# Joined products, sums and small steps on VectorE and GpSimd, and rows and bias added by accumulating DMAs, in a fused autocorrelation-attention and feed-forward kernel

## What is computed

```
x = x + autocorrelation(layernorm(x), ctx, ctx)            # x, ctx: (8, 512, 2048), 8 heads
    # per head and channel:
    qf, kf = fft(q, axis=positions), fft(k, axis=positions)
    corr = ifft(qf * conj(kf)).real
    w, idx = top_k(corr, 12);  w = softmax(w)
    out = sum_i w_i * v[min(idx_i + position, L - 1)]
h = layernorm(x)
out = h @ W.T + bias + sum_e coeffs_e * scales_e * (h @ A_e.T) @ B_e.T      # W: (2048, 2048), 16 experts of rank 16
x = x + out
```

## Time and profile before

| what | value |
|---|---|
| median of 3 runs | 2646.56 us (2642.76 to 2648.35) |
| profiled execution: span of the core | 2644.4 us |
| profiled execution: its own time beyond the span | not shown by the page |
| mean granted TensorE clock | 0.984 |
| DMA | 613.19 MB, 232 GB/s over the span |

### The profile page before, as it was taken

The page is one execution under the profiler, slowest core; times in us unless marked ns, Lnnn a source line. Parts: engine busy times, 40 slices in busy tenths (PEclk is TensorE's granted clock), DMA queues, the critical chain, the costliest instruction groups (busy, mean ns, idle before and its releaser), DMA issues.

```text
span 2644.4 us, 36606 instructions
## 1 busy us (share of the span) xinstructions
PE 2497.7 (94%) x12288; PEld 1559.9 (59%) x12288; DVE 1901.7 (72%) x4966; ACT 1055.7 (40%) x1906; POOL 2155.5 (82%) x1558
## 2 busy tenths in 40 slices
PE   4999866799999999999999999999999999999998
PEld 3655555566666656666666666666666666654444
DVE  5989989778787788777877788778876688645000
ACT  4788855533443343533443334533333233201000
POOL 5799999778998799988998899888998899654222
PEclk8999978899999999999999999999999999999999
DMA  9399998966788687966887687957786687758853
GB/s 325 99 261 269 269 244 198 231 192 209 254 266 228 219 252 238 277 203 210 258 270 210 217 275 248 271 181 236 253 250 172 219 265 243 199 203 301 268 180 114
DMA packets 550028, 613.19 MB, mean 232 GB/s; under 512 B 322640, under 2 KB 448720, under 8 KB 532176
## 3 DMA queue, kind: packets, MB, share of 16 engines
q1 hardware_dynamic: 549840, 610.86, 76.6%
HBM read 383.22 MB, written 151.00 MB: 202 GB/s over the span
## 4 chain that ended last, share of the span: by engine, by line
PE 53%; POOL 22%; DVE 8%; DMA 7%; SPq 5%; issue 4%; ACT 1%; POOLq 0%; DVEq 0%; ACTq 0%
PE f_ps L840 11%; PE f_ps L844 11%; PE f_ps L842 11%; PE a_ps L718 7%; PE a_ps L805 5%; PE a_ps L763 4%; POOL a_zu L1115 4%; POOL f_x1p L1115 4%; POOL a_rows L1115 3%; DMA a_w_lag<-a_w_row 2%; PE a_ps L821 2%; PE a_ps L820 2%; POOL a_zv L1115 2%; POOL a_zf L1115 2%; PE a_ps L768 1%
## 5 line engine op out<-in xcount | busy, mean ns | idle before, releaser
L840 PE MATMUL f_ps<-f_whi,f_hhi 128*128 128x512 f16 x2048 | 777.3, 380 | 5.6 <-issue 2.4
L844 PE MATMUL f_ps<-f_whi,f_hlo 128*128 128x512 f16 x2048 | 777.4, 380 | 0.0
L842 PE MATMUL f_ps<-f_wlo,f_hhi 128*128 128x512 f16 x2048 | 777.4, 380 | 0.0
L924 ACT ACTIVATE a_side<-a_ps 128x256 f32<-128x256 f32 (+1 forms) x320 | 128.0, 416 | 873.5 <-PE a_ps L805 698.4
L844 PEld LDWEIGHTS f_ps<-f_whi,f_hlo 128*128 128x128 f16 x2048 | 200.6, 98 | 242.3 <-issue 1.1
L842 PEld LDWEIGHTS f_ps<-f_wlo,f_hhi 128*128 128x128 f16 x2048 | 200.7, 98 | 230.8 <-issue 1.1
L840 PEld LDWEIGHTS f_ps<-f_whi,f_hhi 128*128 128x128 f16 x2048 | 200.7, 98 | 220.6 <-issue 6.7
L1115 POOL TENSOR_TENSOR a_prod<-a_prod,a_tf 128x512 f32<-128x512 f32 x128 | 160.2, 1273 | 138.7 <-DVE a_tf L1242 138.7
L1115 POOL TENSOR_TENSOR a_zv<-a_zv,a_tw 128x512 f32<-128x512 f32 x128 | 183.3, 1450 | 100.5 <-DVE a_tf L1242 100.5
L805 PE MATMUL a_ps<-inv,a_prod 128*128 128x256 f32 x1024 | 239.5, 388 | 25.6 <-POOL a_prod L1115 25.6
L1115 POOL TENSOR_TENSOR f_x1p<-f_x1p,f_y 128x512 f32<-128x512 f32 x128 | 172.7, 1381 | 101.0 <-DVE f_y L1242 101.0
(11 more groups left out here) (137 smaller groups left out, 5236.6 us busy)
## 6 DMA issues: line engine op xcount, KB each, us to landing
f_whi<-whi_scratch SPq DMA_DIRECT2D x128, 512.0 KB, 5.1
f_wlo<-wlo_scratch SPq DMA_DIRECT2D x128, 512.0 KB, 6.5
a_rows<-in_x_dram SPq DMA_DIRECT2D x62, 1024.0 KB, 8.7
vs<-in_ctx_dram SPq DMA_DIRECT2D x64, 512.0 KB, 6.2
xs<-in_x_dram SPq DMA_DIRECT2D x64, 512.0 KB, 8.0
parts_scratch<-a_so SPq DMA_DIRECT2D x64, 512.0 KB, 7.5
x_scratch<-a_rows SPq DMA_DIRECT2D x32, 1024.0 KB, 5.1
f_x1p<-x_scratch SPq DMA_DIRECT2D x32, 1024.0 KB, 6.8
```

Of the source, the lines that this page charges most:

```text
L840: nc.tensor.matmul(f_ps[:, t, :], h_hi[q][:, kq, rows_t], w_hi[u % WR][:, :, kq, :], start=(k == 0), stop=False)
L842: nc.tensor.matmul(f_ps[:, t, :], h_hi[q][:, kq, rows_t], w_lo[u % WR][:, :, kq, :], start=False, stop=False)
L844: mm = nc.tensor.matmul(f_ps[:, t, :], h_lo[q][:, kq, rows_t], w_hi[u % WR][:, :, kq, :], start=False, stop=(k == DB - 1))
L924: return nc.scalar.activation(out, source, ACT.Copy, **how)
```

## The change

The spectra of values (vk) and of the upper part (uk) are kept side by side in one tile of six blocks, so that one VectorE instruction multiplies a PSUM bank with both halves it is needed for: multiply_queries and multiply_upper issue two products of 1024 elements each in place of four of 512, multiply_lower two of 2048 in place of eight. ScalarE writes the first copy of a spectrum in one instruction with 1024 elements. On GpSimd add_upper loses its raise (the one-partition add of the last row), add_lower adds in two instructions of 1024, raises both parts in one, and adds the halves in one. In largest and choose the small steps over the two halves of a chunk are one instruction each, and each fold of the lags as well; their semaphores count once a chunk. The attn and bias buffers go. add_row and add_bias are DMAs from GpSimd's queue that accumulate into the tile, from parts and from bias in DRAM. x1p and scale have two buffers, and load_group waits for group g-1 where it waited for group g. The core of the diff:

```diff
             def store_x1(w, r):
-                sp.wait_ge(row_added, r + 1)
+                sp.wait_ge(row_added, 16 * (r + 1))
...
-                at_least(sp, y_done, TB * g)
-                sp.dma_start(scale_sb[:, :], wscale[cols].partition_broadcast(T)).then_inc(scale_in, 16)
-                at_least(sp, bias_added, g)
-                sp.dma_start(bias_sb[:, :], bias[cols].partition_broadcast(T)).then_inc(bias_in, 16)
-                at_least(sp, out_out, 16 * g)
+                x1p = x1ps[g % 2]
+                at_least(sp, y_done, TB * (g - 1))
+                sp.dma_start(scales_sb[g % 2][:, :], wscale[cols].partition_broadcast(T)).then_inc(scale_in[g % 2], 16)
+                at_least(sp, out_out, 16 * (g - 1))
...
-                if r is not None and r % TB == 0:
-                    load_attn(r, False)
...
                     store_x1(w, r)
-                    if r % TB < TB - 1:
-                        load_attn(r + 1, True)
...
-                copy(dst[:, 1:3, :], ps[:, 2, :, :])
-                copy(dst[:, 0, :], ps[:, 2, 0, :]).then_inc(moved, 1)
+                copy(dst.rearrange("p (r j) c -> p r j c", j=2)[:, 0:3:2],
+                     ps[:, 2, :, :].unsqueeze(1).broadcast_to([T, 2, 2, CH])).then_inc(moved, 1)
...
             def add_lower(n):
...
+                sums, parts_z = by_pair(z[:, 4:12, :]), by_pair(terms[:, :, :], 6)
+                add(sums[:, :, 0], parts_z[:, :, 0], ALU.add).then_inc(zf_added, 1)
+                add(sums[:, :, 1], parts_z[:, :, 1], ALU.subtract).then_inc(z_paired, 1)
                 pool.wait_ge(zu_added, n + 1)
+                pool.wait_ge(zf_added, n + 1)
                 pool.wait_ge(last_raised, n + 1)
...
+                add(z[0:1, 0:9:8, :], last[n % LB][0:1, :].unsqueeze(1).broadcast_to([1, 2, CH]), ALU.add
+                    ).then_inc(zu_raised, 1)
                 pool.wait_ge(z_paired, n + 1)
                 pool.wait_ge(zu_raised, n + 1)
-                add(zu[:, 0:2, :], zv[:, 0:2, :], ALU.add)
-                add(zu[:, 2:4, :], zv[:, 2:4, :], ALU.add).then_inc(z_added, 1)
+                add(zu, zv, ALU.add).then_inc(z_added, 1)
...
                 pool.wait_ge(rows_in[w % 2], 16 * rows_job(w))
-                pool.wait_ge(attn_in, 16 * (r + r // TB + 2))
-                add(rows[w % 2][:, :], attn[:, :], ALU.add).then_inc(row_added, 1)
+                at_least(pool, row_added, 16 * r)
+                pool.wait_ge(parts_out, 16 * CHUNKS * (r // TB + 1))
+                pool.dma_start(rows[w % 2][:, :], part_rows[r * T:(r + 1) * T, :], accum_op=ALU.add
+                               ).then_inc(row_added, 16)
...
-                pool.wait_ge(x1p_in, 16 * (g + 1))
-                pool.wait_ge(bias_in, 16 * (g + 1))
-                add(x1p[:, :, :], bias_sb[:, :].unsqueeze(1).broadcast_to([T, TB, WC]), ALU.add
-                    ).then_inc(bias_added, 1)
+                cols = slice(g % 4 * WC, (g % 4 + 1) * WC)
+                pool.wait_ge(x1p_in[g % 2], 16 * (g // 2 + 1))
+                pool.dma_start(x1ps[g % 2][:, :, :], bias[cols].partition_broadcast(T).unsqueeze(1).broadcast_to([T, TB, WC]),
+                               accum_op=ALU.add).then_inc(bias_added, 16)
...
+            def product_by_both(out, bank, both):
+                source = ps[:, bank, :, :].rearrange("p j c -> p (j c)").unsqueeze(1).unsqueeze(1)
+                return product(out, source.broadcast_to([T, 2, 2, 2 * CH]),
+                               both.rearrange("p s (r j) c -> p s r (j c)", j=2))
...
             def multiply_lower(n):
...
+                product_by_both(by_pair(z[:, 4:12, :]), 2, both[:, :, 0:4, :]).then_inc(w0_used, 1)
                 dve.wait_ge(w0_mm, 2 * n + 2)
                 dve.wait_ge(prod_added, 2 * min(n + 2, N))
...
+                product_by_both(by_pair(terms[:, :, :], 6), 3, both[:, :, 2:6, :]).then_inc(w0_used, 1)
...
             def choose(n):
...
+                dve.wait_ge(far_copied, SUB * (n + 1))
+                by_lag = ps[:, 0:2, :, :].rearrange("p g h (a l) -> p (g h) a l", a=2)
+                copied = side[:, :, :].rearrange("p g (h l) -> p (g h) l", h=2)
+                near, far = by_lag[:, :, 0, 1:T], by_lag[:, :, 1, 1:T]
+                nc.vector.tensor_tensor(far, near, copied[:, :, 1:T], ALU.subtract)
+                nc.vector.tensor_tensor(near, near, copied[:, :, 1:T], ALU.add).then_inc(lags_folded, 1)
```

More of the change, by code:

```diff
@@ L171, in inverse_root_of_tile, with by_pair @@
         op.then_inc(link, 1)
+def by_pair(tile, every=4):
+    return tile.rearrange("p (s a) c -> p s a c", a=every)[:, :, 0:4, :].rearrange("p s (r j) c -> p s r (j c)", j=2)
 class Shared:
@@ L274, in flow @@
         y = sb("f_y", [T, TB, WC])
-        x1p = sb("f_x1p", [T, TB, WC])
-        scale_sb = sb("f_scale", [T, WC])
-        bias_sb = sb("f_bias", [T, WC])
+        x1ps = [sb(f"f_x1p{i}", [T, TB, WC]) for i in range(2)]
+        scales_sb = [sb(f"f_scale{i}", [T, WC]) for i in range(2)]
         f_bn = sb("f_bn", [T, 4, 6])
@@ L287, in flow @@
         idle = sb("a_idle", [1, 8])
-        tq = sb("a_tq", [T, TB, CH])
         tv = sb("a_tv", [T, TB, CH])
[L290 to L295, removed]
+        spectra = [sb(f"a_spectra{i}", [T, 2, 6, CH]) for i in range(2)]
+        z = sb("a_z", [T, 12, CH])
+        zu, zv, zf = z[:, 0:4, :], z[:, 4:8, :], z[:, 8:12, :]
         tu = sb("a_tu", [T, 4, CH])
-        tw = sb("a_tw", [T, 4, CH])
-        tf = sb("a_tf", [T, 4, CH])
-        term = tf
+        terms = sb("a_terms", [T, 12, CH])
+        prod = terms[:, 4:12, :]
+        tq = terms[:, 0:4, :]
         wts = sb("a_wts", [T, SUB, L])
@@ L425, in flow @@
         y_added = sem("f_y_added")
-        x1p_in = sem("f_x1p_in")
-        scale_in = sem("f_scale_in")
-        bias_in = sem("f_bias_in")
+        x1p_in = [sem(f"f_x1p_in{i}") for i in range(2)]
+        scale_in = [sem(f"f_scale_in{i}") for i in range(2)]
         bias_added = sem("f_bias_added")
@@ L1154, in add_products @@
                 pool.wait_ge(q_used, 2 * (n + 1))
-                add(prod[:, 0:2, :], term[:, 0:2, :], ALU.add).then_inc(prod_added, 1)
-                add(prod[:, 2:4, :], term[:, 2:4, :], ALU.subtract).then_inc(prod_added, 1)
+                add(prod[:, 0:2, :], prod[:, 4:6, :], ALU.add).then_inc(prod_added, 1)
+                add(prod[:, 6:8, :], prod[:, 2:4, :], ALU.subtract).then_inc(prod_added, 1)
             def add_upper(n):
@@ L1318, in choose @@
                                                    ).then_inc(kept, 1)
[L1319 to L1331 removed]
+                dve.wait_ge(kept, SUB * (n + 1))
+                nc.vector.tensor_scalar(total, total, 1.0 / LAG_SCALE, None, ALU.mult).then_inc(total_scaled, 1)
+                dve.wait_ge(total_scaled, n + 1)
+                nc.vector.reciprocal(share, total).then_inc(share_known, 1)
+                dve.wait_ge(far_copied, SUB * (n + 1))
[4 more added lines that the diff above has]
+                nc.vector.tensor_tensor(near, near, copied[:, :, 1:T], ALU.add).then_inc(lags_folded, 1)
             def weights_low(n):
```

110 lines of the change are left out of this document (35 added, 75 removed).

## The result

The changed kernel takes 2775.99 us, the median of 4 runs (2774.88 to 2777.8), beside 2644.66 for the kernel before in the same session: 1.0495 times as long, 95% interval 1.048 to 1.051, or 131 us more. The prediction had said 2664 with a range that ended at 2702. The sign was right, the size was a seventh of what came.

What follows compares the result with a forecast made beforehand. It took a chain of full TensorE windows as the bound, broken by lag matmuls waiting for transposed weights. 2644.4 + 25 - 3 - 3 - 2 = 2661 us of span, 2664 as run median; range 2620 to 2702.

Steps and rivals of the forecast that it cites:

- Part (3): Bias by accumulating DMA: about 11 us of cover before the group add, costed at nothing; GpSimd 1.2 us earlier.
- part (2): VectorE's joined products and sums: nothing net, bound 1.2 us either way in each of the first 12 windows.
- parts (1): GpSimd's small adds joined: 0.5 us less a window, hidden in the middle, 3 us gained over seven early windows.
- Rival C: Bias lands late, after more than 11 us, delaying group add, output matmuls and row: +50 to +80; chance 0.10.
- Part (4): Rows by accumulating DMA: late sum makes TensorE wait 3.1 us in second and fourth row tiles; cost 25 us.
- D: Time from GpSimd reaching the row to the semaphore freeing SyncE and VectorE: 4.5 us before, taken as 9.0.
- Part (5): Ends: 3 us gained from 340 to 490 us, 2 us less after 2300 us.
- the even waits of 3 us at the lags: Expected sign: lag matmuls wait about 3 us each in second and fourth row tiles alike, clock dips behind.
- all of GpSimd's 320 us: Expected sign: GpSimd's busy time falls by some 290 us of row and bias adds and 30 of joined ones.
- waits appear in front of the group add: Sign of being wrong: waits in front of GpSimd's group add, which the bias DMA was expected to precede.
- plain windows change length: Sign of being wrong: windows without a row tile were expected to stay at 36.30 us.
- rivals A: Slower by the late row, landing in about 8.3 to 11 us; up to +52, 2698 us; chance 0.46.

Runs made afterwards that it cites:

- e4: The changed kernel with the bias DMA issued one window earlier: 2716.1 us.
- e1: The changed kernel with the negated maximum and the scaled total as two 128x1 instructions each again: 2745.5 us.
- e7: The kernel before with only the row of the residual added by an accumulating DMA: 2684.5 us.
- e3: The changed kernel with the bias added on GpSimd again from single buffers, rows still by accumulating DMA: 2721.9 us.
- e2: The changed kernel without both accumulating DMAs, rows and bias added on GpSimd as before, everything joined kept: 2685.7 us.
- e13: The changed kernel with the two small steps on 128x1 again and the bias DMA issued one window earlier: 2690.9 us.
- e6: The changed kernel without both accumulating DMAs and with the small steps on 128x1, leaving wide products and joined adds: 2642.0 us.
- e8: The kernel before with the weights' transposes issued ahead of the store of x1 on SyncE: 2665.7 us.
- e5: The kernel before with only the negation and the scaling joined, each once on 128x2: 2888.0 us.
- e10: e6 with the negation and scaling joined to 128x2 as products with a tile of constants: 2715.6 us.
- e9: e7 with the part output placed ahead of the row statistics on VectorE: 2726.7 us.

## Why the prediction was wrong

The 131 us are three shares, each from a run that undoes it: the late bias 62 us (e4), the two small steps 33 (e1), the row's DMA 36 to 47 (e7, e3 against e2, e13 against e6). The wide products and joined adds give back 5 (e6). Part (3) is the largest miss, part (2) the one with the wrong mechanism.

**Part (2), "I set all of (2) at nothing net; the bound is 1.2 us either way", is the step with the wrong mechanism.** It bounded each joined step by the fixed part of an instruction, so joining could save 1.2 us or cost a short delay. The two steps on 128x2 cost 1.7 us in each of the first windows and 33 in all, and alone in the kernel before 241. Its count was high too: twelve and seven instructions less a window, where the page shows 15 in all. The neighbours of the term were right: e6 is at -5 where parts (1) and (2) without these steps gave -3, the joined 128x1024 add takes 2350 ns where 2.35 us were worked out, and the raise of 512 elements 1255 ns where 715 + 500 were.

The trace before did hold the row that I needed, in a group that I had not read. VectorE's row remainder (L1394), in the kernel before, once beside GpSimd and once with its second input in PSUM:
```profile
L1394 DVE TENSOR_TENSOR f_rowlo<-a_rows,f_rowhi x28: 2281/2328/5586, 658.4 to 2458.9; 128x2048 f16<-128x2048 f32 x28
L1394 DVE TENSOR_TENSOR f_rowlo<-a_rows,f_ps x4: 2278/2278/2280, 379.3 to 476.2; 128x2048 f16<-128x2048 f32 x4
```
(least, median and greatest duration in ns.) With an input in PSUM the four take 2278 to 2280; with both inputs in SBUF it goes up to 5586, and in e8 to 13048. One instance on each engine, kernel before:
```profile
1544.51 3.45 DVE L1394 TENSOR_TENSOR f_rowlo<-a_rows,f_rowhi 128x2048 f16<-128x2048 f32 x1
...
1540.87 4.93 POOL L1115 TENSOR_TENSOR f_x1p<-f_x1p,f_y 128x512 f32<-128x512 f32 x4
1545.77 4.54 POOL L1115 TENSOR_TENSOR a_zu<-a_zu,a_tu 128x512 f32<-128x512 f32 x2
```
GpSimd's add ends at 1545.80, and VectorE's operation 2.16 us after that, nearly the 2.28 that it takes alone. GpSimd's next pair takes 4.54 in place of 2.50: it waited in turn. The Trainium skill says why in "SBUF — State Buffer", Who interferes with whom: VectorE and GpSimd share a pair of ports under an exclusive lock. A VectorE operation with two inputs in SBUF contends with a GpSimd instruction that reads SBUF, and one in a two-port mode, which tensor_scalar can enter, takes the pair for its whole length. By that rule the products out of PSUM stay free, and the joined small steps and the row remainder need not. The traces agree with it in e1, e5, e8 and e10. The page has the other engine block while the first one holds the pair; e5 shows VectorE passed over for five GpSimd instructions in a row.

**Part (3), "I cost it at nothing; its cover is gone if it lands later than that", had a cover but no duration.** The cover of about 11 us was near: GpSimd issued at 1064.81 and wanted the sum at 1074.7, 9.9 us. But I gave the bias no landing time, and took its being in time for the likeliest. It lands after 13.8 us. Rival C has exactly this mechanism and price (+50 to +80; measured 62), and I gave it a chance of 0.10 without a duration to weigh. The row's 8.5 us do not hold for it: same bytes, other shape.

**Part (4) had the right D, two thirds of the price, and the wrong place.** D = 9.0 against 8.9 in the tile above and a median of 8.5. +25 against 36 alone. That e7's two waits also grew by 25 us is chance: the prediction's 25 were 19 us of waits and 6 of clock, measured are 25 of waits and 14 of clock. The estimate from the Trainium skill, D near 11 by "Collectives: The Full Stack", is above the medians that the runs show, 8.0 to 9.1; the 7 from "DMA: Bandwidth & Descriptors", in the Trainium skill too, is below them. The wait did not come at the lags, about 3 us in each second and fourth tile, but at the queries, since VectorE's part output is queued behind the statistics. I had named VectorE among those that wait for the row and not asked what is queued behind it there. e9 shows that the lags would have been late as well, so both readings hold, one hiding the other. The clock did dip behind such waits (0.60 at 1110 us).

**Part (5)** took 5 us off at the ends. From 340 to 490 us TensorE's busy time fell from 96.65 to 95.16 though GpSimd's fell by 22, and windows nine to thirteen took 175 us in place of 166, so nothing came back; from the last window's lags to the end the kernel takes 317 us in place of 308.

Of the tests set beforehand, the row's landing came true; the even waits of 3 us at the lags did not, nor did all of GpSimd's 320 us; "waits appear in front of the group add" and "plain windows change length" were named as signs of being wrong, and both came.

The parts moved together, too. I had added them as if only one could be large: rivals A and C happened at once, which the range left out.

## What to carry to other kernels

Before joining small operations of VectorE beside a busy GpSimd, ask where the operands lie and how many elements there are: an operation of 0.15 us with one element in a row took 1.0 to 4.2 on average with two. Look in the trace before for a group of VectorE whose greatest duration is far above its median, and a GpSimd group that is long at the same time. And after any change of order compare the longest instance of such groups before you explain the time by the edit itself: in e8 a change on SyncE lengthened a VectorE instruction from 2.3 to 13 us. An add that is moved into a DMA takes the place of a load made in advance, so that its whole landing is exposed: price it with a duration of its own, issue it a stage early where its inputs allow, and follow the queue behind every engine that waits for it.

## What was not expected of the hardware

- A VectorE operation on 128x2 FP32 in SBUF (with a constant, or two tensors) runs only when GpSimd lets it in: mean 1.0 to 1.5 us in the kernels with wide GpSimd instructions, 4.2 for the negation in e5, up to 10.04 across back-to-back GpSimd instructions. With a constant on 128x1 it takes 0.13 to 0.16, and the reciprocal on 128x2 0.165 to 0.168 in all 64 cases of the changed kernel. A subtraction of two 128x2048 tiles in SBUF, 2.28 us at its shortest, took 13.05 in e8.
- The same two steps cost 241 us with the narrow adds (e5) and 43 with the wide ones (e2 against e6). That the joined GpSimd instructions made the difference is likely from the counts under e5 and not shown, since VectorE's products differ too.
- An accumulating DMA of 1 MB from HBM into SBUF lands after 8.5 us as 128 rows of 8 KB and after 13.8 as 512 pieces of 2 KB from one broadcast row. GpSimd is held for 0.9 and 1.3 us to issue them. Which of the differences makes the second longer was not tried.
